# Moving two casts of the FFN's inner layer and the cast of z on ScalarE, z's low part on VectorE, and the last z to TensorE

## The chip, the cores and the metric

The kernel runs on one core of a Trainium2 chip. The metric is the device time of one execution in microseconds; a lower one is better. Matmuls run on TensorE (PE in the profile), the other work on VectorE (DVE), ScalarE (ACT) and GpSimd (POOL); SyncE (SP) issues all DMAs.

## What is computed

One layer over 128 sequences of 128 rows of 256 features: layer norm, self-attention with 16 heads of 16 features, a second input through its own matrix, a second layer norm, and an FFN with 1024 inner features.

```python
tgt1 = _layer_norm(tgt, g1, be1)
tgt = tgt + _self_attn(tgt1, mask, Wq, bq, Wk, bk, Wv, bv, Wo, bo)
tgt = tgt + (memory @ Wg.T + bg)
tgt1 = _layer_norm(tgt, g2, be2)
ff = jax.nn.relu(tgt1 @ W1.T + b1) @ W2.T + b2
return tgt + ff
```

All of it is in fp32. A product of two fp32 matrices is made from three products of fp32r parts: each operand is cast to a high part (`_hi`), the low part (`_lo`) is the operand minus the high one, and TensorE adds lo*hi, hi*lo and hi*hi.

## The kernel before

The work is cut into 64 groups of two sequences, 256 rows each. It is a software pipeline: pass i of the loop norms group i+2 (`norm`), makes q, k and v of group i+1 (`front`), scores, softmax and transposes of group i (`attn_`), attends and projects group i-1 and norms it again (`out_`), and runs the FFN of group i-2 (`ffn`). Every engine has its own copy of `iteration`, a list of 13 ticks (t = 0 to 12) written out by hand. The order within an engine is the order in which its function issues, and semaphores tie the engines together. SP has a list too, with one queue of DMAs.

The path of z, the normed residual of group g that the FFN reads, in pass i = g+1 (`out_`) and then i = g+2 (`ffn`):

- VectorE at t = 7 adds the residual (L699) and takes its statistics (L604, L611). GpSimd makes the inverse root (`rstd`, L867 and L869). VectorE at t = 8 makes `xhat` (L617, two instructions), and transposes it in blocks of 32x32 into the tile `attn` (L626, two instructions).
- SP moves the blocks back to `xhat` with four DMAs (L392), which completes the transpose.
- ScalarE at t = 12 casts `zT_hi` from `xhat` (L441), ahead of the copy of the transposed inverse sums (L468) and, at t = 0 of the next pass, of the copy of the last turned chunk of probabilities (L460). The first exponentials follow (L448).
- VectorE at t = 0 of the next pass, between the first and the second minima (L725), subtracts to `zT_lo` (L733). TensorE waits for it before the first of four up products.

The path of the inner layer `hid`: each of the four up products (UP_TICKS) is followed by a relu of two halves on ScalarE (L501, RELU_TICKS), a cast to `hT_hi` on VectorE (L684, `hidden_high`, HIDDEN_TICKS 4, 5, 6 and 8), the low part `hT_lo` on GpSimd (L874) and a quarter of the down product on TensorE (DOWN_TICKS, t = 9 to 12). GpSimd has the fourth low part at t = 8, behind `rstd` of the same pass (t = 7) and ahead of `xT_hi` and `xT_lo` (t = 10, L918 and L923), which wait for the DMAs of the turned x (`x_in<-x_quads`, L382).

```python
HIDDEN_TICKS = (4, 5, 6, 8)
RELU_TICKS = (3, 4, 5, 7)
```

On TensorE pass i ends with the transpose of the inverse sums (L1030, t = 12); the text counts periods by it. Then come the scores of the next pass, the last chunk's transposes, q, the values and the first up product. The second up product stands behind the first chunk's transposes (L1022) at t = 3 and waits for the first relu. `x_in` is normed on VectorE by the same form as `xhat` (L617) at t = 5. `mask_bias` (L821) and `sum_inv` (L652) follow at t = 9.

Of the kernel before, what the change touches and what calls it, by code (L numbers as in the profile page):

```python
# [29 lines left out]
ACT = mybir.ActivationFunctionType  # L30
# [38 lines left out]
def xattn_block(nc, x, memory, mask, wqT, wkT, wvT, woT, wgT, w1T, w2T,  # L69
# [26 lines left out]
    with ExitStack() as ctx:  # L96
# [6 lines left out]
        def sem(name):  # L103
            return ctx.enter_context(nc.semaphore(name))
# [62 lines left out]
        for name, n in VECTORS:  # L167
# [56 lines left out]
        proj_ready, xres_biased, resid_ready = sem("proj_ready"), sem("xres_biased"), sem("resid_ready")  # L224
        ln2_stats, ln2_mean, ln2_var, ln2_rstd, ln2_ready = (
            sem(f"ln2_{n}") for n in ("stats", "mean", "var", "rstd", "ready"))
        z_blocked, z_cols, z_hi, z_split = (sem(f"z_{n}") for n in ("blocked", "cols", "hi", "split"))

        hid_ready, hid_relu, hid_hi, hid_split = (sem(f"s_hid_{n}") for n in ("ready", "relu", "hi", "split"))
        down_ready, resid_biased, y_summed = sem("down_ready"), sem("resid_biased"), sem("y_summed")  # L230

        QUADS = P // 32
# [89 lines left out]
        def _(sp):  # L322
# [29 lines left out]
            def iteration(i, norm, front, attn_, out_, ffn):  # L352
# [32 lines left out]
                if known(i, 1, GROUPS):  # L385
                    sp.wait_ge(resid_ready, i)
                    sp.dma_start(x_res[:], x_rows[i]).then_inc(xres_loaded, 16)
                if out_:

                    sp.wait_ge(z_blocked, i)  # L390
                    for n in range(QUADS):
                        sp.dma_start(xhat2_flat[:, n * P:(n + 1) * P],  # L392
                                     attn_blocks[32 * n:32 * (n + 1), :].rearrange("c (j n) -> c j n", j=QUADS)
                                     ).then_inc(z_cols, 16)
# [32 lines left out]
        def _(act):  # L427
# [42 lines left out]
            def iteration(i, norm, front, attn_, out_, ffn):  # L470
                for t in range(TICKS):
                    if out_ and t == 0:
                        copy_turned(i - 1, CHUNKS - 1)
                    if is_at(i, -1) and t == 0:
                        split_high(by_tile[1], xT[0][:], x_turned, 1, v_ready, None, x_hi)
                    if attn_ and t == EXP_TICKS[0]:
# [18 lines left out]
                    if ffn and t in RELU_TICKS:  # L495
                        g, n = i - 2, RELU_TICKS.index(t)
                        act.wait_ge(hid_ready, HJ * g + n + 1)
                        if n >= 2 or later(g):
                            act.wait_ge(hid_split, HJ * g + n - 1)
                        for j in range(2):  # L500
                            last = act.activation(hid[:, n % 2, j, :],  # L501
                                                  up_bank(i, n)[:, j * ROWS:(j + 1) * ROWS],
                                                  ACT.Relu, bias=b1c[:, 2 * n + j:2 * n + j + 1])
                        last.then_inc(hid_relu, 1)
                    if attn_ and t in EXP_TICKS[1:]:
                        exponentials(i, EXP_TICKS.index(t))
                    if attn_ and t in TURN_TICKS and t not in (5, 7):
# [9 lines left out]
                        last.then_inc(k_high, 1)  # L517
                    if attn_ and t in (4, 6, 7, 9):
                        exponentials(i, CPB + (4, 6, 7, 9).index(t))
                    if out_ and t == 12:  # L520
                        g = i - 1
                        split_high(quad_cols(xhat2), in_order(zT[0]), z_cols, 16 * QUADS * (g + 1), hid_ready,
                                   HJ * g if later(g) else None, z_hi)
                    if attn_ and t == 12:
                        copy_inverses(i)

# [16 lines left out]
        def _(dve):  # L543
# [147 lines left out]
            def iteration(i, norm, front, attn_, out_, ffn):  # L691
                for t in range(TICKS):
# [18 lines left out]
                    if attn_ and t < CHUNKS:  # L711
# [15 lines left out]
                                in1=mask_bias[:, b, :], scale=1.0, scalar=HIGHEST, op0=ALU.add,  # L727
                                op1=ALU.min, accum_out=row_min[:, t, h:h + 1])
                        last.then_inc(scores_masked, 1)
                    if ffn and t == 0:  # L730
                        g = i - 2
                        dve.wait_ge(z_hi, g + 1)
                        dve.tensor_tensor(in_order(zT[1]), quad_cols(xhat2), in_order(zT[0]), ALU.subtract  # L733
                                          ).then_inc(z_split, 1)
# [37 lines left out]
                        dve.tensor_copy(attnT[0][:], attn[:]).then_inc(attnT_hi, 1)  # L772
                    if out_ and t == 4:
                        split_low(attn[:], attnT, attnT_hi, i, attnT_split)
                    if ffn and t in HIDDEN_TICKS and t < 8:
                        hidden_high(i - 2, HIDDEN_TICKS.index(t))
                    if norm and t == 4 and i != -1:
                        dve.wait_ge(x_loaded, 16 * (i + 3))
# [25 lines left out]
                    if out_ and t == 8:  # L804
                        g = i - 1
                        if later(g):
                            dve.wait_ge(z_split, g)
                        layer_norm_apply(g, resid, mv2, rstd2, ln2_rstd, xhat2, ln2_ready)
                        dve.wait_ge(attnT_split, g + 1)
                        turn_quads(attn_blocks, xhat2, ln2_ready, g + 1, z_blocked)  # L810
                    if ffn and t == HIDDEN_TICKS[-1]:
                        hidden_high(i - 2, HJ - 1)
                    if front and t == 9:
                        set_values(i + 1, 0)
                        set_values(i + 1, 1)
# [20 lines left out]
        def _(pool):  # L836
# [39 lines left out]
            def iteration(i, norm, front, attn_, out_, ffn):  # L876
                for t in range(TICKS):
                    if norm and t == 5:
                        inverse_root(i + 2, mv1, var1, rstd1, ln1_mean, ln1_var, ln1_ready, ln1_rstd)
                    if ffn and t in HIDDEN_TICKS:  # L880
                        g, n = i - 2, HIDDEN_TICKS.index(t)
                        if n == 0 and later(g):
                            pool.wait_ge(down_ready, g)
                        split_low(hid[:, n % 2], [h[:, 2 * n:2 * n + 2, :] for h in hT], hid_hi,
                                  HJ * g + n + 1, hid_split)
                    if out_ and t == 2:
                        g = i - 1
                        pool.wait_ge(mem_loaded, 16 * (g + 1))
# [40 lines left out]
        def _(pe):  # L929
# [122 lines left out]
            def iteration(i, norm, front, attn_, out_, ffn):  # L1052
                fronts, outs = stages_before(i)
                for t in range(TICKS):
# [60 lines left out]
                        last.then_inc(v_ready, 1)  # L1115
                    if ffn and t in UP_TICKS:
                        up(i, t)
                    if ffn and t in DOWN_TICKS:

                        g, part = i - 2, DOWN_TICKS.index(t)  # L1120
# [57 lines left out]
```

## Time and profile before

| | |
|---|---|
| median of 3 runs | 1758.4 us (1757.55 to 1760.98) |
| profiled execution | 1759.22 us, its span 1757.3 us |
| TensorE, matmul | 1684.2 us busy, 96% |
| VectorE | 1509.3 us, 86% |
| ScalarE | 1393.1 us, 79% |
| GpSimd | 953.5 us, 54% |
| DMA, queue of SP | 41.5% of 16 engines' span |

Busy is the union of an engine's instructions over the span; a busy TensorE is not one at its peak, since matmuls overlap. In a timeline a row gives the start and the length in us, the engine, the line, what is written <- what is read, and how many instructions were merged (x4); in brackets the idle time of the engine before it and what ended it. DVE, ACT, POOL and SPq stand for VectorE, ScalarE, GpSimd and SyncE's queue. The granted clock of TensorE was 0.99 of full speed over the span.

### The profile page before, as it was taken

What the parts mean: (1) busy time and instruction counts of PE and PEld (TensorE: products, weight loads), DVE (VectorE), ACT (ScalarE), POOL (GpSimd) and SP (SyncE); (2) the same over time, 40 slices, a digit from 0 to 9 for tenths busy, and PEclk for the clock granted to TensorE, in tenths of its full rate; (3) what the DMA queues carried; (4) which work ended last, traced back from release to release, by engine and by line L of the source; (5) the groups of instructions that cost most, each with busy time, mean ns of one, the idle gap of its engine ahead of it and who ended that gap; (6) DMA issues with size and microseconds to landing.
All of it is one profiled execution on the core that took longest, in us unless ns stands there. A gap on an engine that the chain in (4) does not pass through costs nothing. (4 is left out here: it accounts for less than half of the span.)

```text
span 1757.3 us, 53486 instructions
## 1 busy us (share of the span) xinstructions
PE 1684.2 (96%) x17272; PEld 1643.0 (93%) x17272; DVE 1509.3 (86%) x7136; ACT 1393.1 (79%) x5506; POOL 953.5 (54%) x906
## 2 busy tenths in 40 slices
PE   6799999999999999999999999999999999999997
PEld 5699999999999999999999999999999999999997
DVE  7798898898888888888888888888888888888873
ACT  4788788788788788788788788788788787787782
POOL 5355545545545545555555555555555555555544
PEclk8899999999999999999999999999999999999999
DMA  5434444444444444444444444444444444444421
GB/s 187 130 124 138 140 131 138 131 139 132 134 142 130 137 140 130 136 141 131 136 145 128 136 142 131 135 142 132 134 139 136 133 141 135 128 146 135 128 91 37
DMA packets 258951, 233.77 MB, mean 133 GB/s; under 512 B 26992, under 2 KB 209136, under 8 KB 258672
## 3 DMA queue, kind: packets, MB, share of 16 engines
q1 hardware_dynamic: 258672, 230.35, 41.5%
q8 instruction: 139, 2.28, 0.6%
q14 instruction: 140, 1.15, 0.2%
HBM read 62.73 MB, written 16.78 MB: 45 GB/s over the span
## 5 line engine op out<-in xcount | busy, mean ns | idle before, releaser
L448 ACT ACTIVATE scores<-scores,row_min 128x128 f32<-128x128 f32 x2048 | 799.5, 406 | 37.1 <-DVE row_min L725 37.1
L874 POOL TENSOR_TENSOR hT_lo<-hid,hT_hi 128x512 fp32r<-128x512 f32 x256 | 339.6, 1327 | 687.7 <-DVE hT_hi L684 687.7
L725 DVE CUSTOM_DVE_ANT_0 scores<-score_ps,mask_bias 128x128 f32<-128x128 f32 x2048 | 467.8, 286 | 1.5 <-issue 1.1
L448 ACT ACTIVATION_READ_ACCUMULATOR scores<-scores,row_min 128x1 f32 x2048 | 420.5, 205 | 0.0
L460 ACT ACTIVATE probs<-turn_ps 128x512 f32<-128x512 f32 x512 | 306.3, 599 | 92.6 <-PE turn_ps L1022 92.6
L956 PE MATMUL ffn_ps<-w_hi,hT_lo 128*128 128x256 f32 x1024 | 301.2, 294 | 32.6 <-POOL hT_lo L874 32.2
L1022 PE MATMUL turn_ps<-ident,scores 128*128 128x128 f32 x2048 | 307.1, 273 | 5.3 <-ACT probs L460 5.3
L956 PE MATMUL ffn_ps<-zT_hi,w_lo 128*128 128x256 f32 x992 | 294.0, 296 | 1.4 <-ACT hid L501 1.2
L958 PE MATMUL ffn_ps<-w_hi,hT_hi 128*128 128x256 f32 x1024 | 284.2, 277 | 0.0
L957 PE MATMUL ffn_ps<-w_lo,hT_hi 128*128 128x256 f32 x1024 | 283.5, 277 | 0.0
L957 PE MATMUL ffn_ps<-zT_lo,w_hi 128*128 128x256 f32 x992 | 276.1, 278 | 0.0
L958 PE MATMUL ffn_ps<-zT_hi,w_hi 128*128 128x256 f32 x992 | 275.5, 278 | 0.0
L501 ACT ACTIVATE hid<-ffn_ps,vec 128x256 f32<-128x256 f32 x496 | 208.6, 481 | 43.9 <-PE ffn_ps L958 43.8
L1022 PEld LDWEIGHTS turn_ps<-ident,scores 128*128 128x128 f32 x2048 | 235.2, 140 | 6.1 <-ACT scores L448 6.1
L956 PEld LDWEIGHTS ffn_ps<-w_hi,hT_lo 128*128 128x128 f32 x1024 | 192.4, 188 | 47.3 <-POOL hT_lo L874 46.6
L1008 PE MATMUL score_ps<-k_stack,q_stack 128*128 128x256 f32 x1024 | 206.7, 294 | 2.3 <-DVE row_min L725 2.3
L956 PEld LDWEIGHTS ffn_ps<-zT_hi,w_lo 128*128 128x128 f32 x992 | 187.2, 189 | 14.6 <-issue 12.3
L957 PEld LDWEIGHTS ffn_ps<-w_lo,hT_hi 128*128 128x128 f32 x1024 | 193.0, 189 | 0.0
L958 PEld LDWEIGHTS ffn_ps<-w_hi,hT_hi 128*128 128x128 f32 x1024 | 192.3, 188 | 0.0
L957 PEld LDWEIGHTS ffn_ps<-zT_lo,w_hi 128*128 128x128 f32 x992 | 187.0, 188 | 0.0
L958 PEld LDWEIGHTS ffn_ps<-zT_hi,w_hi 128*128 128x128 f32 x992 | 186.3, 188 | 0.0
L725 DVE DVE_READ_ACCUMULATOR2_ANT row_min<- 128x1 f32 x2048 | 168.9, 82 | 0.0
(144 smaller groups left out, 4288.0 us busy)
## 6 DMA issues: line engine op xcount, KB each, us to landing
q_stack<-q_hi SPq DMA_DIRECT2D x128, 256.0 KB, 2.4
k_stack<-k_hi SPq DMA_DIRECT2D x256, 128.0 KB, 2.3
x_in<-x_dram SPq DMA_DIRECT2D x64, 256.0 KB, 2.7
mem_in<-memory_dram SPq DMA_DIRECT2D x64, 256.0 KB, 3.0
x_res<-x_dram SPq DMA_DIRECT2D x64, 256.0 KB, 3.0
q_stack<-q_lo SPq DMA_DIRECT2D x64, 256.0 KB, 2.3
k_stack<-k_lo SPq DMA_DIRECT2D x128, 128.0 KB, 2.3
inv<-inv_cols SPq DMA_DIRECT2D x256, 64.0 KB, 2.4
```

The source lines that it names most:

```text
L448: last = act.activation(exps, exps, ACT.Exp, bias=row_min[:, k, h:h + 1], scale=-1.0, accum_out=row_sum[:, k, h:h + 1])
L460: act.activation(probs[:, k, :], turn_ps[k % 2][:, :], ACT.Copy).then_inc(probs_copied[k % 2], 1)
L501: last = act.activation(hid[:, n % 2, j, :], up_bank(i, n)[:, j * ROWS:(j + 1) * ROWS], ACT.Relu, bias=b1c[:, 2 * n + j:2 * n + j + 1])
L725: last = dve.tensor_tensor_reduce(out=scores[:, slot(i, t), h, :], in0=score_ps[t % 2][:, h * S:(h + 1) * S], in1=mask_bias[:, b, :], scal ...
L874: pool.tensor_tensor(halves[1], src, halves[0], ALU.subtract).then_inc(done, 1)
L956: pe.matmul(dst, lhs[1], rhs[0], start=start and j == 0, stop=False, **more)
L957: pe.matmul(dst, lhs[0], rhs[1], start=False, stop=False, **more)
L958: last = pe.matmul(dst, lhs[0], rhs[0], start=False, stop=stop and j == n - 1, **more)
L1008: last = pe.matmul(score_ps[n % 2][:, k * 2 * S:(k + 1) * 2 * S], q_stack[i % 2][:, c, k, seq(b)], k_stack[i % 2][:, c, :, GB * k + b, :], ...
L1022: last = pe.transpose(turn_ps[k % 2][:, h * S:(h + 1) * S], scores[:, slot(g, k), h, :], ident[:])
```

## The change

Four parts. (a) ScalarE casts `zT_hi` at t = 0 of the pass in which the FFN reads it, behind the copy of the last turned chunk, instead of at t = 12 of the pass before. (b) VectorE makes `zT_lo` at t = 1, behind the second minima, instead of t = 0. (c) The third and fourth `hT_hi` are cast by ScalarE right behind their relus, and GpSimd's low parts wait for them by a semaphore of their own. (d) The z of the last group is turned by TensorE from `xhat` into a PSUM bank, ahead of the last quarter of the down product; its parts are taken from there, and its block transposes and DMAs are left out.

```diff
--- before.py
+++ after.py
@@ -224,9 +224,11 @@
         proj_ready, xres_biased, resid_ready = sem("proj_ready"), sem("xres_biased"), sem("resid_ready")
         ln2_stats, ln2_mean, ln2_var, ln2_rstd, ln2_ready = (
             sem(f"ln2_{n}") for n in ("stats", "mean", "var", "rstd", "ready"))
+        z_turned = sem("z_turned")
         z_blocked, z_cols, z_hi, z_split = (sem(f"z_{n}") for n in ("blocked", "cols", "hi", "split"))
 
         hid_ready, hid_relu, hid_hi, hid_split = (sem(f"s_hid_{n}") for n in ("ready", "relu", "hi", "split"))
+        hid_late_hi = sem("s_hid_late_hi")
         down_ready, resid_biased, y_summed = sem("down_ready"), sem("resid_biased"), sem("y_summed")
 
         QUADS = P // 32
@@ -385,7 +387,7 @@
                 if known(i, 1, GROUPS):
                     sp.wait_ge(resid_ready, i)
                     sp.dma_start(x_res[:], x_rows[i]).then_inc(xres_loaded, 16)
-                if out_:
+                if out_ and i < GROUPS:
 
                     sp.wait_ge(z_blocked, i)
                     for n in range(QUADS):
@@ -471,6 +473,12 @@
                 for t in range(TICKS):
                     if out_ and t == 0:
                         copy_turned(i - 1, CHUNKS - 1)
+                    if is_at(i, GROUPS + 1) and t == 0:
+                        split_high(by_tile[1], zT[0][:], z_turned, 1, hid_ready, HJ * (GROUPS - 1), z_hi)
+                    elif ffn and t == 0:
+                        g = i - 2
+                        split_high(quad_cols(xhat2), in_order(zT[0]), z_cols, 16 * QUADS * (g + 1), hid_ready,
+                                   HJ * g if later(g) else None, z_hi)
                     if is_at(i, -1) and t == 0:
                         split_high(by_tile[1], xT[0][:], x_turned, 1, v_ready, None, x_hi)
                     if attn_ and t == EXP_TICKS[0]:
@@ -502,6 +510,10 @@
                                                   up_bank(i, n)[:, j * ROWS:(j + 1) * ROWS],
                                                   ACT.Relu, bias=b1c[:, 2 * n + j:2 * n + j + 1])
                         last.then_inc(hid_relu, 1)
+                        if n >= 2:
+                            act.wait_ge(hid_relu, HJ * g + n + 1)
+                            act.activation(hT[0][:, 2 * n:2 * n + 2, :], hid[:, n % 2], ACT.Copy
+                                           ).then_inc(hid_late_hi, 1)
                     if attn_ and t in EXP_TICKS[1:]:
                         exponentials(i, EXP_TICKS.index(t))
                     if attn_ and t in TURN_TICKS and t not in (5, 7):
@@ -517,10 +529,6 @@
                         last.then_inc(k_high, 1)
                     if attn_ and t in (4, 6, 7, 9):
                         exponentials(i, CPB + (4, 6, 7, 9).index(t))
-                    if out_ and t == 12:
-                        g = i - 1
-                        split_high(quad_cols(xhat2), in_order(zT[0]), z_cols, 16 * QUADS * (g + 1), hid_ready,
-                                   HJ * g if later(g) else None, z_hi)
                     if attn_ and t == 12:
                         copy_inverses(i)
 
@@ -727,7 +735,9 @@
                                 in1=mask_bias[:, b, :], scale=1.0, scalar=HIGHEST, op0=ALU.add,
                                 op1=ALU.min, accum_out=row_min[:, t, h:h + 1])
                         last.then_inc(scores_masked, 1)
-                    if ffn and t == 0:
+                    if is_at(i, GROUPS + 1) and t == 1:
+                        split_low(by_tile[1], zT, z_hi, GROUPS, z_split)
+                    elif ffn and t == 1:
                         g = i - 2
                         dve.wait_ge(z_hi, g + 1)
                         dve.tensor_tensor(in_order(zT[1]), quad_cols(xhat2), in_order(zT[0]), ALU.subtract
@@ -772,7 +782,7 @@
                         dve.tensor_copy(attnT[0][:], attn[:]).then_inc(attnT_hi, 1)
                     if out_ and t == 4:
                         split_low(attn[:], attnT, attnT_hi, i, attnT_split)
-                    if ffn and t in HIDDEN_TICKS and t < 8:
+                    if ffn and t in HIDDEN_TICKS[:2]:
                         hidden_high(i - 2, HIDDEN_TICKS.index(t))
                     if norm and t == 4 and i != -1:
                         dve.wait_ge(x_loaded, 16 * (i + 3))
@@ -806,10 +816,9 @@
                         if later(g):
                             dve.wait_ge(z_split, g)
                         layer_norm_apply(g, resid, mv2, rstd2, ln2_rstd, xhat2, ln2_ready)
-                        dve.wait_ge(attnT_split, g + 1)
-                        turn_quads(attn_blocks, xhat2, ln2_ready, g + 1, z_blocked)
-                    if ffn and t == HIDDEN_TICKS[-1]:
-                        hidden_high(i - 2, HJ - 1)
+                        if i < GROUPS:
+                            dve.wait_ge(attnT_split, g + 1)
+                            turn_quads(attn_blocks, xhat2, ln2_ready, g + 1, z_blocked)
                     if front and t == 9:
                         set_values(i + 1, 0)
                         set_values(i + 1, 1)
@@ -881,8 +890,8 @@
                         g, n = i - 2, HIDDEN_TICKS.index(t)
                         if n == 0 and later(g):
                             pool.wait_ge(down_ready, g)
-                        split_low(hid[:, n % 2], [h[:, 2 * n:2 * n + 2, :] for h in hT], hid_hi,
-                                  HJ * g + n + 1, hid_split)
+                        split_low(hid[:, n % 2], [h[:, 2 * n:2 * n + 2, :] for h in hT],
+                                  hid_hi if n < 2 else hid_late_hi, 2 * g + n % 2 + 1, hid_split)
                     if out_ and t == 2:
                         g = i - 1
                         pool.wait_ge(mem_loaded, 16 * (g + 1))
@@ -1115,6 +1124,10 @@
                         last.then_inc(v_ready, 1)
                     if ffn and t in UP_TICKS:
                         up(i, t)
+                    if is_at(i, GROUPS) and t == 12:
+                        pe.wait_ge(ln2_ready, GROUPS)
+                        pe.wait_ge(resid_ready, GROUPS)
+                        turn(by_tile[1], xhat2).then_inc(z_turned, 1)
                     if ffn and t in DOWN_TICKS:
 
                         g, part = i - 2, DOWN_TICKS.index(t)
```

How it moves instructions on ScalarE, in a steady pass, from the second exponentials behind the last relu to the first ones of the next pass (`hid` is the relu's output, `probs<-turn_ps` the copy of a turned chunk). Before:

```order
L501 ACTIVATE hid<-ffn_ps,vec 128x256 x2
L448 ACTIVATE scores,row_sum<-scores,row_min 128x128 x4
L460 ACTIVATE probs<-turn_ps 128x512
L448 ACTIVATE scores,row_sum<-scores,row_min 128x128 x4
L460 ACTIVATE probs<-turn_ps 128x512 x2
L441 ACTIVATE zT_hi<-xhat 128x512
L468 ACTIVATE inv_cols<-turn_ps 128x128
L460 ACTIVATE probs<-turn_ps 128x512
L448 ACTIVATE scores,row_sum<-scores,row_min 128x128 x4
```

Of the change:

```order
L509 ACTIVATE hid<-ffn_ps,vec 128x256 x2
L515 ACTIVATE hT_hi<-hid 128x512
L450 ACTIVATE scores,row_sum<-scores,row_min 128x128 x4
L462 ACTIVATE probs<-turn_ps 128x512
L450 ACTIVATE scores,row_sum<-scores,row_min 128x128 x4
L462 ACTIVATE probs<-turn_ps 128x512 x2
L470 ACTIVATE inv_cols<-turn_ps 128x128
L462 ACTIVATE probs<-turn_ps 128x512
L443 ACTIVATE zT_hi<-xhat 128x512
L450 ACTIVATE scores,row_sum<-scores,row_min 128x128 x4
```

`hT_hi` now stands behind the relu, and `zT_hi` behind the copies instead of ahead of them.

On VectorE the end of a pass, from the eighth minima on (left out) to the last sum. Before:

```order
L617 SCALAR_TENSOR_TENSOR xhat<-resid,mv,rstd 128x256 x2
L626 STREAM_TRANSPOSE attn<-xhat 128x2x4x32 x2
L684 CAST hT_hi<-hid 128x512
L666 TENSOR_TENSOR v_pad<-work_ps,row 128x8x16 x4
L821 TENSOR_SCALAR mask_bias<-mask_in 128x256
L652 RECIPROCAL sum_inv<-row_sum 128x32 x2
L709 TENSOR_TENSOR y<-ffn_ps,resid_b 128x512
```

Of the change:

```order
L625 SCALAR_TENSOR_TENSOR xhat<-resid,mv,rstd 128x256 x2
L634 STREAM_TRANSPOSE attn<-xhat 128x2x4x32 x2
L674 TENSOR_TENSOR v_pad<-work_ps,row 128x8x16 x4
L830 TENSOR_SCALAR mask_bias<-mask_in 128x256
L660 RECIPROCAL sum_inv<-row_sum 128x32 x2
L717 TENSOR_TENSOR y<-ffn_ps,resid_b 128x512
```

The fourth `hT_hi` is gone from behind the transposes. On GpSimd nothing changes its place: the fourth `hT_lo` stands behind `rstd` and ahead of `xT_hi` in both.

## Rows read from the trace of the kernel before

**Rows 1.** Waits, whole run: engine line waited for: us in total, times, longest us.

```profile
PE ffn_ps L956 <- POOL hT_lo L874: 32.2, 61, 1.2
```

**Rows 2.** Timeline of TensorE, one period: start us, us, engine line op.

```profile
1059.33 0.27 PE L1030 MATMUL turn_ps<-ident,sum_inv 128*128 128x128 f32 x1
...
1067.37 0.60 PE L1022 MATMUL turn_ps<-ident,scores 128*128 128x128 f32 x4
...
1067.72 0.37 PE L956 MATMUL ffn_ps<-zT_hi,w_lo 128*128 128x256 f32 x1
...
1084.25 0.39 PE L956 MATMUL ffn_ps<-w_hi,hT_lo 128*128 128x256 f32 x1 [0.48 <-POOL hT_lo L874]
...
1085.73 0.27 PE L1030 MATMUL turn_ps<-ident,sum_inv 128*128 128x128 f32 x1
```

**Rows 3.** Timeline of TensorE, start and end of a later period.

```profile
1667.43 0.27 PE L1030 MATMUL turn_ps<-ident,sum_inv 128*128 128x128 f32 x1
...
1693.09 0.27 PE L1030 MATMUL turn_ps<-ident,sum_inv 128*128 128x128 f32 x1
```

**Rows 4.** Timeline of VectorE, the period of rows 2.

```profile
1060.99 1.22 DVE L733 TENSOR_TENSOR zT_lo<-xhat,zT_hi 128x512 fp32r<-128x512 f32 x1
...
1070.76 0.84 DVE L788 SCALAR_TENSOR_TENSOR k_lo<-work_ps,qk_bias,k_hi 128x256 fp32r<-128x256 f32 x2
...
1077.16 0.36 DVE L684 CAST hT_hi<-hid 128x512 fp32r<-128x512 f32 x1
...
1077.44 0.68 DVE L699 TENSOR_TENSOR resid<-work_ps,x_res 128x512 f32<-128x512 f32 x1
...
1080.39 0.88 DVE L617 SCALAR_TENSOR_TENSOR xhat<-resid,mv,rstd 128x256 f32<-128x256 f32 x2 [0.26 <-POOL rstd L869]
...
1081.37 1.16 DVE L626 STREAM_TRANSPOSE attn<-xhat 128x256 f32<-128x256 f32 x2
```

**Rows 5.** Timeline of GpSimd, the same period.

```profile
1061.63 1.48 POOL L891 TENSOR_TENSOR memT_hi<-mem_in,one 128x512 fp32r<-128x512 f32 x1
...
1079.59 0.69 POOL L869 TENSOR_TENSOR rstd<-var,minus_half 128x2 f32<-128x2 f32 x1
...
1082.92 1.27 POOL L874 TENSOR_TENSOR hT_lo<-hid,hT_hi 128x512 fp32r<-128x512 f32 x1 [2.64 <-DVE hT_hi L684]
...
1084.15 1.09 POOL L918 TENSOR_TENSOR xT_hi<-x_in,one 128x512 fp32r<-128x512 f32 x1
```

**Rows 6.** Timeline of ScalarE, the same period, and its next zT_hi.

```profile
1060.20 0.63 ACT L441 ACTIVATE zT_hi<-xhat 128x512 fp32r<-128x512 f32 x1 [2.20 <-DMA xhat<-attn]
...
1060.73 0.26 ACT L468 ACTIVATE inv_cols<-turn_ps 128x128 f32<-128x128 f32 x1
...
1061.37 0.40 ACT L448 ACTIVATE scores<-scores,row_min 128x128 f32<-128x128 f32 x1
...
1066.70 0.83 ACT L501 ACTIVATE hid<-ffn_ps,vec 128x256 f32<-128x256 f32 x2
...
1069.43 0.84 ACT L515 ACTIVATE k_hi<-work_ps,qk_bias 128x256 fp32r<-128x256 f32 x2
...
1086.60 0.63 ACT L441 ACTIVATE zT_hi<-xhat 128x512 fp32r<-128x512 f32 x1 [2.20 <-DMA xhat<-attn]
```

**Rows 7.** Tile x_in on VectorE, 300 to 1600 us: durations ns min/median/max.

```profile
L617 DVE SCALAR_TENSOR_TENSOR x_in<-x_in,mv,rstd x98: 475/994/1528, 304.9 to 1575.6; 128x256 f32<-128x256 f32 x98
```

**Rows 8.** Timeline of GpSimd and VectorE, around 76 us.

```profile
75.94 1.26 POOL L923 TENSOR_TENSOR xT_lo<-x_in,xT_hi 128x512 fp32r<-128x512 f32 x1
...
76.04 1.31 DVE L821 TENSOR_SCALAR mask_bias<-mask_in 128x256 f32<-128x256 f32 x1
```

**Rows 9.** Timeline of SyncE's queue, the same period.

```profile
1076.07 2.56 SPq L382 DMA_DIRECT2D x_in<-x_quads  x4
```

**Rows 10.** Timeline of TensorE, near the end.

```profile
1738.11 0.28 PE L958 MATMUL ffn_ps<-w_hi,hT_hi 128*128 128x256 f32 x1
...
1741.12 0.38 PE L956 MATMUL score_ps<-zT_hi,w_lo 128*128 128x256 f32 x1 [2.74 <-DVE zT_lo L733]
```

## The prediction

> **What bounds the kernel now.** I read the waits first, then the timelines of one period, engine by engine. The waits show one thing that stops TensorE in nearly every pass of the loop over i: the last quarter of the FFN's low parts, hT_lo from GpSimd, 32.2 us in 61 waits [rows 1]. A period is one pass of that loop, from one transpose of the inverse sums on TensorE to the next: 1059.33 to 1085.73, 26.40 us [rows 2]. Between 1059.33 and 1667.43 there are 23 of them, mean 26.44 [rows 2, 3]. The reader should see in the timeline that the wait falls before the last quarter of the down product [rows 2], and that GpSimd's hT_lo before it starts late because VectorE casts the last hT_hi only behind the two transposes of xhat (they end at 1082.53, hT_lo starts at 1082.92) [rows 4, 5]. A period without that wait is on show: 1667.43 to 1693.09, 25.66 us [rows 3]. So TensorE's floor is 25.66, and taking the wait away is worth at most 0.74 us a period.
>
> TensorE is not the only cycle. Follow z: ScalarE casts zT_hi at 1060.20, comes to the first exponentials at 1061.37, and, with no idle between, to the end of k_hi at 1070.27 [rows 6]. VectorE takes k_lo at 1070.76 and works through to the end of the xhat transposes at 1082.53, its one pause the 0.26 us before xhat, for rstd [rows 4]. The four DMAs and their landing take 4.07 us more, to the next zT_hi at 1086.60 [rows 6]. Here ScalarE runs 0.5 us ahead of k_lo, so this cycle does not bind yet.
>
> **The change, part by part.**
> (1) Two casts leave VectorE. The third cast costs 1077.44 - 1077.16 = 0.28 us and stands before xhat [rows 4]: the z cycle gets 0.28 shorter. The fourth stands behind the transposes and shortens only what follows there. On ScalarE a cast of this shape is 0.53, by zT_hi's 1060.20 to 1060.73 [rows 6], plus some 0.1 because it waits for the relu just before it. Both lie behind k_hi, so not on the z cycle, and ScalarE waits 2.20 us for the DMA at the period's end [rows 6], which covers twice 0.63. The third and fourth hT_lo are then ready long before TensorE asks: the wait on hT_lo goes [rows 1].
> (2) zT_hi moves behind the copies of inverses and of the last chunk. The cycle from zT_hi to k_hi loses the 0.64 between 1060.73 and 1061.37 [rows 6]. It becomes 0.53 + (1070.27 - 1061.37 = 8.90) + a hand-over of about 0.1 + (1082.53 - 1070.76 = 11.77) - 0.28 + 4.07 = 25.1 us, below TensorE's floor. The inverse copy, and the DMAs behind it, come no later than now.
> (3) zT_lo moves behind the second minima. It takes 1.22 from 1060.99 now [rows 4]. TensorE needs it for the first up product, and the z cycle waits for zT_hi, not for zT_lo. So I cost the move at nothing: if it came late, TensorE would stand before the first up product instead of before the second, for the same time. If one of GpSimd's low parts got in first, it would be some 1.3 us later still; that bound goes into the upper end.
> (4) The order on GpSimd does not change, but its waits do, and here I find the price. Now GpSimd idles 2.64 us between rstd and the fourth hT_lo [rows 5], and VectorE does xhat, two instructions with two SBUF inputs, in 0.88 undisturbed [rows 4]. After the change hT_hi is ready before rstd ends, so hT_lo starts straight behind rstd, just when xhat starts. The same form on x_in shows what that costs: alone 0.475, but up to 1.528 when an hT_lo runs beside it [rows 7]. The extra is about the whole GpSimd instruction, so one shuts the other out.
> Who is first? VectorE starts xhat 0.11 after rstd's end (1080.28 to 1080.39) [rows 4, 5]; GpSimd goes on without a pause where nothing holds it (1082.92 + 1.27 = 1084.19, next start 1084.15) [rows 5]. This race was run once, at 76 us: GpSimd 0.10 ahead, its instruction unhurt at 1.26, VectorE's mask_bias 1.31 [rows 8]. So I take GpSimd first. Then hT_lo runs 1.27 from 1079.96 to 1081.23 (all 0.28 earlier than now), the first xhat ends about 0.28 later, 1081.51. Behind hT_lo in GpSimd's queue stands xT_hi. It needs the x_quads DMAs, issued 1076.07 to 1078.63 [rows 9]; with about 2.5 us of landing from the last one's issue at 1078.0 it is ready near 1080.5, at times later. It then waits at the port while the first xhat runs, and gets in before the second: the waiting side gets the next turn, as zT_lo got it before memT_hi (memT_hi took 1.48 where its like, xT_hi, takes 1.09) [rows 4, 5]. xT_hi holds it for about 0.9, and the second xhat ends at 1082.69. Undisturbed and 0.28 earlier it would be 1080.99. The block c is 1.70 us. Where xT_hi's data come too late, c is 0.92.
> The Trainium skill, SBUF — State Buffer, "Who interferes with whom", says that a VectorE instruction with two SBUF inputs and a GpSimd one that reads SBUF exclude each other for a whole instruction, and that issue order decides who waits. By that rule alone the price is one hT_lo, c near 1.0, and the sum would be that of the first rival below; it says nothing of who is next among waiting ones. This speaks against the change, and the trace agrees with its exclusion (1.528 against 0.475).
> (5) The period is then the larger of two: 25.1 + c, and TensorE with half of (c - 0.28) added to 25.66 (the second up product starts at 1067.72, 0.35 behind the transposes before it, and waits for the first relu, which ends at 1067.53: a late zT_hi has 0.15 to spare, then stops TensorE there [rows 2, 6]; as TensorE's own lateness makes the next z earlier by its clock, half of it counts). With c = 1.70: 26.80 against 26.37. With c = 0.92: 26.02. I take the long block in five periods of six: 26.67, and 0.05 for the irregular periods that the mean of 26.44 has over 26.40: 26.72. That is 0.28 longer than now, over the 59 periods between the passes with all stages (i = 2 to 61), +16.5 us.
> (6) The end. The last z skips transposes and DMAs. TensorE now idles from the last down matmul at 1738.11 to 1741.12, 3.0 us [rows 10]. New: y and zT_lo, two of the form of resid, 0.68 each [rows 4], with hand-overs about 1.8. The longest wait for hT_lo, 1.2 [rows 1], goes too, and four transposes cost 0.35. Gain 2 us; I keep 0 and 4 as its ends.
>
> Sum: +16.5 - 2 = +14.5. The profiled execution took 1759.22 us (its span of 1757.3 and 1.9 around it), 0.8 above the median 1758.4; from the median I get **1773**.
>
> **Rivals.**
> *VectorE wins the race, or the second xhat follows the first at once.* Then c is 1.03 (0.475, hT_lo's 1.15 behind it, 0.28): period 26.13 + 0.05, 0.26 shorter than now, -15 - 2: about 1741, faster. For: on x_in VectorE went first and lost only one turn. Against: there it had a lead, here GpSimd has. It decides from a lead of about 0.1 us, and the point of no gain is c = 1.3. Chance 0.22.
> *No block.* If xhat is not held up, or only a little, TensorE's floor rules at about 25.75: -0.69 x 59 - 2 = -43, 1715. Against: 1.528 beside 0.475 [rows 7]. Chance 0.06.
> *A mixture.* If the race goes either way from period to period, c averages 1.2 to 1.4 and the time stays within 0.2% (3.5 us, about what a measurement of this kernel can tell from no change): 1755 to 1762. Chance 0.08.
> *More than I count.* Always the long block gives 26.85, +24, and if a late zT_lo also stands behind GpSimd's memT_lo some periods lose more: up to 1786. This is the upper end of the likeliest case.
>
> **How the numbers follow.** My forecast, the double block, has 0.64, and its own range is 1764 to 1786. The 8-in-10 range has to take in the first rival too, so it reaches from 1738 to 1786. Slower gets 0.62 (the forecast, less a little for its edge), same 0.10, faster 0.28 (the two other rivals).
>
> **What would show it.** Right: xhat's two instructions take about 2.6 us instead of 0.88, with an xT_hi of GpSimd between them; the wait on hT_lo is gone from TensorE's list and replaced by waits on the relu in front of the second up product, and on sum_inv; k_lo waits for k_hi on VectorE; ScalarE waits for the xhat DMA before zT_hi, behind the copy of the last chunk; the period is 26.6 to 26.9. First rival: the two take about 1.9 us and the period is 26.1. Wrong altogether: xhat still takes 0.88, or hT_lo does not follow rstd, or the period is ruled by something that I hold to be covered, such as zT_lo or the exponentials behind the two new casts.

## The result and the profile after

The changed kernel takes 1777.3 us (median of 4 runs, 1774.8 to 1780.3) against 1759.7 for the kernel before on the same chip (1757.6 to 1761.0): ratio 1.0102, 95% interval 1.0081 to 1.0123. It is slower by 17.6 us. The profiled execution took 1780.27, its span is 1778.5; it is the longest of the four. Of the experiments' executions one, of the ten of experiment 4, was slow (2778.8 us at a granted clock of 0.56), and its ratio leaves that one out. The rows below are read in the order of the prediction's steps.

The waits of the changed kernel: engine, line, what it waited for, us in total, times, longest. They answer to [rows 1].

```profile
PE ffn_ps L965 <- ACT hid L509: 34.8, 57, 1.4
PE ffn_ps L965 <- DVE zT_lo L743: 10.3, 27, 1.6
ACT zT_hi L443 <- DMA xhat<-attn: 46.1, 55, 2.2
DVE zT_lo L743 <- ACT zT_hi L443: 44.9, 57, 2.2
DVE k_lo L798 <- ACT k_hi L527: 21.7, 39, 2.0
```

TensorE no longer waits for hT_lo. It waits for the first relu, in nearly as many passes, and in some passes for zT_lo: it has become a follower of z. VectorE now waits for k_hi and for zT_hi, as it must if the z cycle binds.

One cycle of z, timelines of four engines (start us, us, engine, line, op). TensorE's transposes of the inverse sums mark the periods, as in [rows 2]:

```profile
1073.10 0.33 PE L1039 MATMUL turn_ps<-ident,sum_inv 128*128 128x128 f32 x1
...
1082.43 0.38 PE L965 MATMUL ffn_ps<-zT_hi,w_lo 128*128 128x256 f32 x1 [0.69 <-ACT hid L509]
```

ScalarE, to the next zT_hi, as in [rows 6]:

```profile
1075.68 0.63 ACT L443 ACTIVATE zT_hi<-xhat 128x512 fp32r<-128x512 f32 x1 [0.70 <-DMA xhat<-attn]
...
1084.29 0.82 ACT L527 ACTIVATE k_hi<-work_ps,qk_bias 128x256 fp32r<-128x256 f32 x2
...
1102.46 0.63 ACT L443 ACTIVATE zT_hi<-xhat 128x512 fp32r<-128x512 f32 x1 [0.68 <-DMA xhat<-attn]
```

VectorE, as in [rows 4]:

```profile
1085.15 0.88 DVE L798 SCALAR_TENSOR_TENSOR k_lo<-work_ps,qk_bias,k_hi 128x256 fp32r<-128x256 f32 x2 [0.53 <-ACT k_hi L527]
...
1094.50 2.61 DVE L625 SCALAR_TENSOR_TENSOR xhat<-resid,mv,rstd 128x256 f32<-128x256 f32 x2 [0.26 <-POOL rstd L878]
1097.22 1.19 DVE L634 STREAM_TRANSPOSE attn<-xhat 128x256 f32<-128x256 f32 x2
```

GpSimd, as in [rows 5]:

```profile
1093.71 0.69 POOL L878 TENSOR_TENSOR rstd<-var,minus_half 128x2 f32<-128x2 f32 x1
1094.36 1.29 POOL L883 TENSOR_TENSOR hT_lo<-hid,hT_hi 128x512 fp32r<-128x512 f32 x1
1095.61 1.22 POOL L927 TENSOR_TENSOR xT_hi<-x_in,one 128x512 fp32r<-128x512 f32 x1
1096.91 1.36 POOL L932 TENSOR_TENSOR xT_lo<-x_in,xT_hi 128x512 fp32r<-128x512 f32 x1
```

The cycle adds up from these rows. From zT_hi (1075.68) to the end of k_hi (1085.11) it is 9.43; the hand-over to k_lo takes 0.04; from k_lo (1085.15) to the end of the transposes (1098.41) 13.26; DMAs and landing to the next zT_hi (1102.46) 4.05. Together 26.78. Inside stands xhat's pair, 2.61 where [rows 4] have 0.88. GpSimd starts hT_lo at 1094.36, 0.14 before xhat; xT_hi follows at 1095.61 and shuts the second xhat out once more.

A pass in which xT_hi's data came too late for the second turn, timeline of VectorE:

```profile
800.07 1.83 DVE L625 SCALAR_TENSOR_TENSOR xhat<-resid,mv,rstd 128x256 f32<-128x256 f32 x2 [0.26 <-POOL rstd L878]
```

and of TensorE, the period that follows it, 831.46 - 805.32 = 26.14:

```profile
805.32 0.27 PE L1039 MATMUL turn_ps<-ident,sum_inv 128*128 128x128 f32 x1
...
831.46 0.33 PE L1039 MATMUL turn_ps<-ident,sum_inv 128*128 128x128 f32 x1
```

The end of both kernels: the idle stretch and the up product of the last z, in windows (us, busy time and count of PE, PEld, DVE, ACT, POOL, granted clock, DMA share, GB/s). Before, the two windows after [rows 10]'s last matmul:

```profile
1738.39:1741.12 2.73, 0.00 (x1) 0.00 (x1) 1.99 (x2) 0.63 (x1) 1.26 (x1) 1.00 0.34 114
1741.12:1748.30 7.18, 7.18 (x48) 7.18 (x49) 1.14 (x3) 2.52 (x6) 2.44 (x2) 0.76 0.00 0
```

After:

```profile
1762.30:1763.80 1.50, 0.17 (x2) 0.00 (x0) 1.29 (x2) 0.00 (x0) 0.45 (x1) 1.00 0.00 0
1763.80:1769.40 5.60, 5.55 (x48) 5.55 (x49) 1.21 (x2) 2.68 (x7) 2.88 (x3) 1.00 0.13 47
```

The pause is shorter, and the up product behind it takes 5.6 us instead of 7.2. Before, TensorE had waited 1.23 us for hT_lo and, 1.65 us of matmuls later, stood 2.74 us; in the up product behind that the granted clock was 0.76 in the mean (in part the lower of the two levels, 1.2 GHz). After, the wait for hT_lo is gone, the pause is 1.38 us, and the clock stayed at 1.00.

### The profile page after: what moved, and what is told of

Same layout as the page of the kernel before. It is cut to its first block and busy times, and to the rows that moved or that the text cites. A ratio compares the mean times of both kernels' runs of the same rounds, so it can differ in the third digit from the quotient of the medians.

```text
span 1778.5 us, 53488 instructions
## 1 busy us (share of the span) xinstructions
PE 1694.2 (95%) x17276; PEld 1641.7 (92%) x17276; DVE 1554.0 (87%) x7006; ACT 1479.6 (83%) x5634; POOL 964.3 (54%) x906
## 5 line engine op out<-in xcount | busy, mean ns | idle before, releaser
L462 ACT ACTIVATE probs<-turn_ps 128x512 f32<-128x512 f32 x512 | 302.0, 591 | 121.3 <-PE turn_ps L1031 121.3
L450 ACT ACTIVATION_READ_ACCUMULATOR scores<-scores,row_min 128x1 f32 x2048 | 398.0, 194 | 0.0
L625 DVE SCALAR_TENSOR_TENSOR xhat<-resid,mv,rstd 128x256 f32<-128x256 f32 x128 | 158.0, 1273 | 17.2 <-POOL rstd L878 17.1
```

What stands on the lines that cost most here:

```text
L450: last = act.activation(exps, exps, ACT.Exp, bias=row_min[:, k, h:h + 1], scale=-1.0, accum_out=row_sum[:, k, h:h + 1])
L462: act.activation(probs[:, k, :], turn_ps[k % 2][:, :], ACT.Copy).then_inc(probs_copied[k % 2], 1)
L625: last = dve.scalar_tensor_tensor(out=dst[:, b, :], in0=src[:, b, :], scalar=mv[:, b, 0:1], in1=rstd[:, b:b + 1].broadcast_to([P, D]), op0 ...
```

## The experiments

**1. The low parts wait for xhat.** After the changed kernel, on GpSimd before the fourth hT_lo:

```diff
+                        if n == HJ - 1 and out_:
+                            pool.wait_ge(ln2_ready, i)
                         split_low(hid[:, n % 2], [h[:, 2 * n:2 * n + 2, :] for h in hT],
```

> The changed kernel with one wait more: GpSimd's fourth hT_lo (and xT_hi behind it in the queue) waits until xhat is written. My theory (the two GpSimd instructions that get in front of xhat's two lengthen the z cycle): xhat's pair goes from 2.60 us back to about 0.88, the cycle is 25.1 us and TensorE's 25.66 rules, the period comes to 25.75 and the time to about 1715 us, 1708 to 1725. Rival A (the work added to ScalarE, or z's later place on it, costs the time, and the long xhat is only slack): 1770 to 1785, no gain, with VectorE waiting elsewhere. Rival B (GpSimd has no room for the delay: hT_lo then comes too late for the last down product): the wait on hT_lo is back in TensorE's list at 0.5 us a period and more, and the time is 1745 or above.

Measured: 1714.9 us (1713.7 to 1715.0), ratio 0.9752, 0.9736 to 0.9768. GpSimd's timeline in it:

```profile
1054.60 0.69 POOL L878 TENSOR_TENSOR rstd<-var,minus_half 128x2 f32<-128x2 f32 x1
1056.35 1.30 POOL L883 TENSOR_TENSOR hT_lo<-hid,hT_hi 128x512 fp32r<-128x512 f32 x1 [1.06 <-DVE xhat L625]
```

VectorE's:

```profile
1055.39 0.88 DVE L625 SCALAR_TENSOR_TENSOR xhat<-resid,mv,rstd 128x256 f32<-128x256 f32 x2 [0.26 <-POOL rstd L878]
```

and TensorE's:

```profile
1034.71 0.27 PE L1041 MATMUL turn_ps<-ident,sum_inv 128*128 128x128 f32 x1
...
1060.45 0.27 PE L1041 MATMUL turn_ps<-ident,sum_inv 128*128 128x128 f32 x1
```

The pair is back at 0.88, the period is 25.74, and ScalarE's wait for the z DMA is gone from the waits. One wait on GpSimd takes 62 us off the changed kernel and 43 off the kernel before. Both rivals fall: with the casts on ScalarE the period is at TensorE's floor, so they cost nothing here, and TensorE has no wait for hT_lo, which therefore has the room.

**2. Only the second turn is taken away.** The same wait, before xT_hi and not before hT_lo:

```diff
                         pool.wait_ge(v_ready, g)
+                        if out_:
+                            pool.wait_ge(ln2_ready, i)
                         pool.tensor_tensor(in_order(xT[0]), quad_cols(x_in),
```

> The changed kernel with one wait more: GpSimd's xT_hi waits until xhat is written, the fourth hT_lo does not. So one GpSimd instruction can get in front of xhat's pair and not two. My theory: the pair takes 1.8 to 1.9 us instead of 2.60, the period is 26.0 to 26.2, the time about 1738 us, 1730 to 1746. Rival (one turn of the port is all the cost there is, the second is hidden behind something else): 1770 to 1780, as the change. Rival (xT_hi's delay makes the next projections late): TensorE waits on xT_hi, and the time is over 1750.

Measured: 1740.4 us (1739.0 to 1743.6), ratio 0.9902, 0.9887 to 0.9917. VectorE's timeline:

```profile
1072.41 1.83 DVE L625 SCALAR_TENSOR_TENSOR xhat<-resid,mv,rstd 128x256 f32<-128x256 f32 x2 [0.26 <-POOL rstd L878]
```

Each turn has its own price: 0.78 us of the pair and 37 us of the run for xT_hi's, 0.95 and 25.5 for hT_lo's (experiment 1). hT_lo's turn is cheaper for the run, since TensorE's own 25.74 takes over before all of it is gained.

**3. The casts alone**, in the kernel before (the two hunks of the diff on ScalarE's casts and `hid_late_hi`, and VectorE's and GpSimd's that belong to them).

> The kernel before with the two late casts on ScalarE alone; zT_hi and zT_lo stay where they were, and the last z keeps its DMAs. My theory: the z cycle keeps the 0.64 us of copies in front of the exponentials' side and gets the double block: 25.1 + 0.64 + 1.70 = 27.4 us a period, 59 periods of 0.7 to 1.0 more than before: 1800 to 1820 us, slower than the change. Rival (z's later place is what costs, the casts are harmless or help): 1760 or less.

Measured: 1824.4 us (1818.2 to 1826.7), ratio 1.0372, 1.0348 to 1.0395; periods of 27.36 in the mean. The period is as the theory has it, the median 4 us above its range. The profiled execution, the fastest of the four, lies inside it; 4 us of its length stand outside the periods (2.3 up to the fourth transpose of inverse sums, 1.8 behind the last), which I had not counted. z's new place is no culprit: with the new end it saves the change 47 us.

**4. The casts back on VectorE**, in the changed kernel (ScalarE's two casts and the semaphore of their own, which go with them, are not shown):

```diff
-                    if ffn and t in HIDDEN_TICKS[:2]:
+                    if ffn and t in HIDDEN_TICKS and t < 8:
...
+                    if ffn and t == HIDDEN_TICKS[-1]:
+                        hidden_high(i - 2, HJ - 1)
```

> The changed kernel with the third and fourth casts back on VectorE; z's later place and the last z on TensorE stay. My theory: hT_lo starts behind the transposes again, xhat's pair takes 0.88, TensorE's wait on hT_lo is back with some 0.5 us a period, the period is 26.4, and the time 1752 to 1762, as before or up to 4 us less for the end. Rival (z's later place costs by itself): 1770 or more.

Measured: 1754.8 us (median of 10), ratio 0.9979, 0.9970 to 0.9989. TensorE's wait for hT_lo is back, as the waits show:

```profile
PE ffn_ps L963 <- POOL hT_lo L881: 22.4, 60, 0.7
```

and xhat is undisturbed, by its tile (durations ns min/median/max):

```profile
L621 DVE SCALAR_TENSOR_TENSOR xhat<-resid,mv,rstd x128: 475/482/486, 73.4 to 1731.6; 128x256 f32<-128x256 f32 x128
```

So the whole loss comes in with the two casts, and z's place plus the new end are worth 3.4 us without them.

**5. The same cycle, shortened elsewhere.** In the changed kernel, before the second hT_lo:

```diff
+                        if n == 1 and norm:
+                            pool.wait_ge(ln1_ready, i + 3)
```

> The changed kernel with one wait more, elsewhere on the same cycle: GpSimd's second hT_lo waits until the normalised x is written, so it can't get in front of VectorE's x_in; xhat stays as blocked as in the change. My theory (what counts is the length of the z cycle, 25.1 + 1.70, wherever a piece of it lies): x_in takes 0.475 instead of 1.528, the cycle is 25.75, at TensorE's floor, the period is 25.8 to 25.95 and the time 1717 to 1728 us, though xhat's pair still takes 2.6. Rival (what costs is the lateness of xhat's block, near the end of the period, and an earlier gain on VectorE is eaten by a wait for TensorE or ScalarE before xhat): 1765 or more.

Measured: 1719.7 us (1719.2 to 1723.9), ratio 0.9790, 0.9773 to 0.9808. The time is as the theory has it, one detail is not: xhat's pair takes 2.6 in only about 3 passes of 10 and 1.83 in the others, because GpSimd's xT_hi now mostly waits for its DMA (44 times by the waits, 9 in the change). The passes with the long pair still tell the two theories apart. Here is one on VectorE:

```profile
876.91 2.61 DVE L625 SCALAR_TENSOR_TENSOR xhat<-resid,mv,rstd 128x256 f32<-128x256 f32 x2 [0.26 <-POOL rstd L878]
```

and the period behind it on TensorE:

```profile
883.12 0.27 PE L1041 MATMUL turn_ps<-ident,sum_inv 128*128 128x128 f32 x1
...
908.90 0.27 PE L1041 MATMUL turn_ps<-ident,sum_inv 128*128 128x128 f32 x1
```

The period is 25.78, where the change has 26.78 behind the same block. x_in had given the cycle its microsecond back. Its tile on VectorE, 300 to 1560 us, where [rows 7] have a median of 994 and a longest of 1528:

```profile
L625 DVE SCALAR_TENSOR_TENSOR x_in<-x_in,mv,rstd x98: 472/477/482, 301.3 to 1542.8; 128x256 f32<-128x256 f32 x98
```

It is the length of the cycle that counts, not where the block lies.

**6. Both waits together.**

> The waits of e1_low_waits_xhat and of e6_low2_waits_x together. My theory: with the first the z cycle is some 0.5 us below TensorE's floor of 25.74 already, so the second gives nothing: the same time as e1_low_waits_xhat, 1715 within 2 us. Rival (e1_low_waits_xhat is still held by the z cycle and not by TensorE): below 1705.

Measured: 1714.0 us (1712.0 to 1714.9), ratio 0.9749, 0.9734 to 0.9764: the same as experiment 1 within the intervals. TensorE's 25.74 to 25.77 a period is the bound, and a shorter z cycle brings no more.

**7. What z's place is worth without the block**: the kernel of experiment 3 with the wait of experiment 1.

> The kernel before with the two late casts on ScalarE and the wait of e1_low_waits_xhat; zT_hi and zT_lo stay in their old places and the last z keeps its DMAs. It tells what z's new place is worth once the block is gone. My theory: the z cycle is 25.1 + 0.64 = 25.74, just TensorE's floor, so the period is 25.75 to 25.9 and the time 1719 to 1730 us (4 us of it the old end). Rival (z's place matters as much without the block as with it, 0.6 us a period): 1750 or more.

Measured: 1727.9 us (1725.2 to 1728.4), ratio 0.9824, 0.9807 to 0.9842. Its periods are 25.92 in the mean: the move is worth about 0.16 us a period there, some 9 us, and the old end the rest of the 12.9 between this and experiment 1. It matters less than with the block, but it is not nothing.

**8. Who comes first: a first try.** Two memsets of 128x2 on GpSimd, in the changed kernel, between rstd and the fourth hT_lo:

```diff
+                        if n == HJ - 1 and out_:
+                            pool.memset(spare1[:], 0.0)
+                            pool.memset(spare2[:], 0.0)
```

> The changed kernel with two memsets of 128x2, 0.1 us each, on GpSimd between rstd and the fourth hT_lo, so that VectorE starts the first xhat about 0.1 us before hT_lo can. My theory (whoever is first has its whole instruction, and the waiting side gets the next turn): the first xhat takes 0.48, hT_lo runs behind it, the second xhat behind that, and xT_hi waits for it; the pair takes about 2.0 us and not 2.6, the period is 26.0 to 26.2, the time 1732 to 1745. Rival (GpSimd's two waiting instructions both get in before the second xhat, whoever starts first): 1770 or more. Rival (VectorE's second follows its first at once, and hT_lo stands behind both): 1715.

Measured: 1780.4 us (1777.7 to 1782.1). The time is the first rival's and outside my range, but GpSimd's timeline shows that the condition was not met:

```profile
1094.73 0.10 POOL L895 MEMSET spare<- 128x2 f32 x1
1094.77 0.10 POOL L896 MEMSET spare<- 128x2 f32 x1
1094.83 1.28 POOL L884 TENSOR_TENSOR hT_lo<-hid,hT_hi 128x512 fp32r<-128x512 f32 x1
```

VectorE's, beside it:

```profile
1094.89 2.67 DVE L626 SCALAR_TENSOR_TENSOR xhat<-resid,mv,rstd 128x256 f32<-128x256 f32 x2 [0.26 <-POOL rstd L879]
```

Memsets of 0.10 us started 0.04 to 0.06 apart, so hT_lo was still 0.06 ahead of xhat. The run tells nothing of VectorE going first.

**9. Who comes first: with a real lead.** The two memsets are waited for:

```diff
+                        if n == HJ - 1 and out_:
+                            for m in range(2):
+                                pool.memset(spare[:], 0.0).then_inc(lead, 1)
+                                pool.wait_ge(lead, 2 * g + m + 1)
```

> As e8b_small_lead, whose two memsets overlapped (hT_lo started only 0.07 us later and was still ahead of xhat): here each of the two memsets is waited for, as rstd waits for var, whose starts lie 0.27 apart with 0.19 for var itself, so hT_lo should start about 0.2 us after the first xhat has started and before it has ended. My theory (whoever is first has its whole instruction, the waiting side gets the next turn): the first xhat takes 0.48, hT_lo runs behind it, the second xhat behind hT_lo, and xT_hi behind that; the pair takes 1.9 to 2.1 us, the period is 26.0 to 26.2, the time 1732 to 1745. Rival (GpSimd's two instructions both get in before the second xhat, whoever is first): 1770 or more. Rival (the second xhat follows the first at once and hT_lo waits for both): the pair takes 0.9, and the time is 1715 to 1720, as with the wait.

Measured: 1744.6 us (1739.4 to 1746.6), ratio 0.9927, 0.9910 to 0.9943. VectorE's timeline:

```profile
1070.05 1.91 DVE L627 SCALAR_TENSOR_TENSOR xhat<-resid,mv,rstd 128x256 f32<-128x256 f32 x2 [0.26 <-POOL rstd L880]
```

The two instructions of that row by their tile (durations ns min/median/max):

```profile
L627 DVE SCALAR_TENSOR_TENSOR xhat<-resid,mv,rstd x2: 486/998/1510, 1070.1 to 1070.5; 128x256 f32<-128x256 f32 x2
```

GpSimd's timeline:

```profile
1070.23 1.45 POOL L885 TENSOR_TENSOR hT_lo<-hid,hT_hi 128x512 fp32r<-128x512 f32 x1
1071.65 1.22 POOL L933 TENSOR_TENSOR xT_hi<-x_in,one 128x512 fp32r<-128x512 f32 x1
```

The first xhat is unhurt (486 ns), hT_lo waits for it and takes 1.45, the second xhat waits for hT_lo (1510 ns), and xT_hi comes behind both. A start 0.32 us later on GpSimd (0.18 behind xhat's start instead of 0.14 ahead) makes the kernel 33 us faster than the change. This is the first rival of the prediction, built on purpose: its forecast was a pair of 1.91 and 1741 us.

**10. zT_lo in front of the second minima again.**

```diff
-                    elif ffn and t == 1:
+                    if ffn and t == 0 and not is_at(i, GROUPS + 1):
```

> The changed kernel with zT_lo back in front of the second minima, zT_hi in its new place. In the change VectorE stands 0.8 us for zT_hi before zT_lo, so zT_lo can't start earlier in front of the minima either; the second minima come later instead. My theory (the length of the z cycle decides, and on it lies zT_hi, not zT_lo or those minima): the same time within 5 us, 1773 to 1783. Rival (the place of zT_lo is what the change loses by, since TensorE waits for it before the up product): 1765 or less. Rival (the second minima have no slack, and the exponentials behind them carry the delay into k_hi): 1790 or more.

Measured: 1787.9 us (1782.6 to 1790.7), ratio 1.0168, 1.0148 to 1.0189, some 10 us above the change. That is outside my forecast and 2 us short of the last rival's. VectorE there stands longer for zT_hi, by the waits:

```profile
DVE zT_lo L743 <- ACT zT_hi L443: 89.6, 63, 2.9
```

It is 44.9 us in the change. The trace shows that the last rival's path carries the delay. One pass on VectorE, where GpSimd's memT_lo starts 0.01 us ahead of zT_lo:

```profile
1240.22 1.83 DVE L743 TENSOR_TENSOR zT_lo<-xhat,zT_hi 128x512 fp32r<-128x512 f32 x1 [1.52 <-ACT zT_hi L443]
```

and on ScalarE, whose second exponentials wait for the second minima behind that zT_lo:

```profile
1242.93 0.41 ACT L450 ACTIVATE scores<-scores,row_min 128x128 f32<-128x128 f32 x1 [0.49 <-DVE row_min L733]
```

From zT_hi to the end of k_hi this pass takes 10.05 us, where the change has 9.43. In 19 of the 59 passes zT_lo takes over 1.5 us, and there it is 9.83 to 10.05; where zT_lo takes 0.69 it is 9.44. That is some 10 us of the run on the z cycle. In the profiled execution, the fastest of the four, most of it is made up for, since 13 passes have the single block and not 5 and fewer transfers came late; its span is 2.4 us longer than the change's. zT_lo's new place is no cause of the loss: behind the second minima it keeps a blocked zT_lo off the cycle.

## Why the prediction was right

Forecast 1773, measured 1777.3, within the range and slower as forecast.

Steps (1) and (2), the casts and the z cycle without the block: 9.43 and 4.05 against 9.43 and 4.07 forecast; the hand-over was 0.04 for 0.1. Experiments 1 and 7 bear out the 25.1: with it TensorE's floor rules, and with 0.64 more it nearly does (25.74 and 25.92 a period).

Step (3), zT_lo at nothing: its wait holds TensorE 27 times for 10.3 us, in part where GpSimd's memT_lo got in first. That bound, which I had put into the upper end, was met in 20 of the 59 passes. In this one GpSimd's memT_lo starts at 1344.80, and zT_lo on VectorE takes 1.82 us and not 0.69:

```profile
1344.82 1.82 DVE L743 TENSOR_TENSOR zT_lo<-xhat,zT_hi 128x512 fp32r<-128x512 f32 x1 [0.65 <-ACT zT_hi L443]
```

On ScalarE, in the same pass:

```profile
1344.15 0.63 ACT L443 ACTIVATE zT_hi<-xhat 128x512 fp32r<-128x512 f32 x1 [0.68 <-DMA xhat<-attn]
...
1352.77 0.83 ACT L527 ACTIVATE k_hi<-work_ps,qk_bias 128x256 fp32r<-128x256 f32 x2
```

From zT_hi to the end of k_hi it is 9.45, as in every other pass (9.43 to 9.45, whether zT_lo was blocked or not). So a late zT_lo adds nothing to the cycle here: nothing was the right price, and the few us that the upper end had for it were not needed. Experiment 10 shows that this hangs on its place behind the second minima.

Step (4), the block: forecast c = 1.70, measured 2.61 - 0.88 = 1.73; 0.92 for the single one, measured 0.95. The order was as argued, hT_lo first, then xT_hi before the second xhat. The long block came in 53 of the 59 passes with all stages, where I took five in six, that is 49. Experiments 1, 2 and 9 remove each turn by itself. By the Trainium skill, SBUF — State Buffer, section "Who interferes with whom", issue order decides who waits. Experiment 9 agrees: a shift of 0.32 us turned 2.61 into 1.91. The sentence gives one turn; that the waiting side is next, and so a second turn is paid, stands in the rows only.

Step (5), the period: forecast 26.80, measured 26.73 to 26.82 in 34 of the 59; behind a single block forecast 26.02, measured 25.91 to 26.25. What failed in size is the term for irregular passes, 0.05 us. From 134.13 to 1718.64 on TensorE are 59 periods, 26.86 in the mean and not 26.72: 8 us in this execution, some 3 of them by more long blocks than I took. In 11 of these cycles the DMAs and their landing took over 4.2 us, together 7.8 us more than the usual 4.06, and all six periods over 27.4 us stand behind such a one (4.74 to 5.61). Here is one. On VectorE the transposes of xhat end at 1044.14:

```profile
1042.96 1.18 DVE L634 STREAM_TRANSPOSE attn<-xhat 128x256 f32<-128x256 f32 x2
```

and on ScalarE zT_hi starts at 1048.88:

```profile
1048.88 0.63 ACT L443 ACTIVATE zT_hi<-xhat 128x512 fp32r<-128x512 f32 x1 [1.37 <-DMA xhat<-attn]
```

The DMAs took 4.74 us this time, 0.69 more than in the cycle above, and the period that began at 1045.64 is 27.46. Before, the z cycle had half a microsecond to spare, and small delays went mostly into that: a landing 0.6 late made the period 0.2 longer, but the latest, 1.3 late, made it 1.2 longer. With the two waits of experiment 6 it has more to spare, and there no period between those with all stages is over 25.8. A cycle that binds pays for each late transfer. There were also fewer before, 4 that took over 4.2 us; why the change has 11 stays open.

Step (6), the end: forecast -2, ends 0 and 4, measured -4.5 (from TensorE's last transpose of inverse sums to the end 39.9 before and 35.4 after). The pause before the last up product shrank by 1.4 and the wait for hT_lo by 1.2, as worked out; what I left out is the clock, 1.6 us in the up product behind the pause. With 0.35 for the four transposes that is 3.9; the other 0.6 was not followed up.

The two misses of size partly cancel, which is luck: +8 for the periods, -2.5 for the end; the beginning (up to the fourth transpose of inverse sums) is 1.1 longer. From +14.5 this gives +21.1, the difference of the two spans. The other three runs of the change are shorter, hence 17.6 between the medians. Of the 4.3 us between forecast and result, 1.3 are the kernel before, which I had at 1758.4 and which measured 1759.7 beside the change.

## What to carry to other kernels

Making an input ready earlier can start a low-priority instruction in front of a critical one. Before you move work so that another engine stops waiting, ask what it will do with its freedom and against whom. Where two engines shut each other out for whole instructions, an explicit wait that lets the short critical pair go first can be worth more than the move itself: here it made of a loss of 17.6 us a gain of 43.

And sum each loop-carried cycle end to end. Its length against the floor tells what a block costs, wherever it lies, and its slack tells how much of every late DMA will show.

## What the runs showed that was not expected

Small independent instructions on GpSimd can overlap so far that they are hardly a delay: two memsets of 0.10 us moved the next start by 0.08 us, while the same two, each waited for, moved it by 0.32.

The pauses of TensorE at the end cost more than their own length, by the clock behind them: 48 matmuls took 7.2 us at a granted clock of 0.76 behind the pauses of 1.2 and 2.7 us of the kernel before, and 5.6 at 1.00 behind the change's pause of 1.4. The kernels of experiments 3 and 7 keep the old end and have one longer pause there, 4.7 and 3.6 us. Their windows of the up product behind it, with a granted clock of 0.65 and 0.79:

```profile
1799.02:1807.50 8.48, 8.48 (x50) 8.48 (x51) 0.85 (x2) 2.97 (x7) 2.57 (x2) 0.65 0.00 0
1710.55:1717.72 7.17, 7.17 (x50) 7.17 (x51) 1.07 (x2) 2.98 (x7) 2.40 (x2) 0.79 0.00 0
```

In all kernels with the new end the pause is 1.38 us and the clock behind it 1.00.
